# Sorting by source in three regions instead of two: the sums of tiles 124 to 255 beside the scatter

## The reference

```python
edge_aggr = zeros.at[row].add(edge_attr).at[col].add(edge_attr)   # layer 0: by source and by destination
agg = jax.ops.segment_sum(edge_attr, col, num_segments=N)         # layer 1: by destination
deg = jax.ops.segment_sum(ones, dst, num_segments=N)              # layers 2 and 3: counts
```

## Time and profile before

| | us |
|---|---|
| median of 3 runs | 1297.22 (1295.68 to 1298.08) |
| the profiled execution | 1292.79 |
| its span, first to last instruction | 1290.9 |
| PE busy | 1191.1 (92%) |
| DVE busy | 886.6 (69%) |
| POOL busy | 695.7 (54%) |
| ACT busy | 658.3 (51%) |

### The profile page before, as it was taken

The page is one execution under the profiler, slowest core; times in us unless marked ns, Lnnn a source line. Parts: engine busy times, 40 slices in busy tenths (PEclk is TensorE's granted clock), DMA queues, the critical chain, the costliest instruction groups (busy, mean ns, idle before and its releaser), DMA issues. The chain is left out here.

```text
span 1290.9 us, 34734 instructions
## 1 busy us (share of the span) xinstructions
PE 1191.1 (92%) x10908; PEld 1027.0 (80%) x10909; DVE 886.6 (69%) x3055; ACT 658.3 (51%) x1751; POOL 695.7 (54%) x720
## 2 busy tenths in 40 slices
PE   6999888999999999678986999997999999999997
PEld 3666556888988888567864999855999999999986
DVE  7999686667777677677778753473667766766753
ACT  8666447777778775379632310051333333333332
POOL 4777777777777777700000000037677777777740
PEclk9999898999999999989998999987999999999997
DMA  8663334454454447168860000058888988888830
GB/s 250 209 224 102 104 110 123 120 145 132 132 142 127 128 130 205 54 177 241 259 41 39 1 2 2 1 162 206 205 214 207 230 211 208 214 209 220 207 93 29
DMA packets 249761, 187.56 MB, mean 145 GB/s; under 512 B 44682, under 2 KB 226433, under 8 KB 249441
## 3 DMA queue, kind: packets, MB, share of 16 engines
q1 hardware_dynamic: 214650, 135.70, 40.9%
q0 software_dynamic: 22656, 46.87, 12.2%
q10 hardware_dynamic: 12264, 2.70, 1.1%
HBM read 139.64 MB, written 43.62 MB: 142 GB/s over the span
## 5 line engine op out<-in xcount | busy, mean ns | idle before, releaser
L2504 POOL DMA_INDIRECT between<-p_table,src_g x292 | 285.7, 978 | 407.9 <-DMA p_table<-n_nm 308.5
L929 POOL DMA_INDIRECT rows_by_block<-h_t,mean_bc x312 | 303.9, 974 | 105.3 <-issue 88.0
L444 PE MATMUL acc<-ones_b 128*128 128x128 bf16 (+1 forms) x2024 | 226.6, 257 | 31.8 <-PEq L864 17.5
L1049 DVE TENSOR_TENSOR between<-between,acc 128x600 f32 x208 | 161.7, 778 | 115.9 <-PE acc L1154 105.8
L2646 ACT ACTIVATE between<-acc 128x384 f32<-128x384 f32 (+2 forms) x156 | 72.6, 465 | 253.9 <-PE acc L2768 199.7
L444 PEld LDWEIGHTS acc<-ones_b 128*128 128x128 bf16 x2024 | 134.1, 99 | 60.8 <-issue 42.5
L1143 PE MATMUL acc<-n_nm 128*128 128x384 bf16 (+1 forms) x832 | 142.8, 295 | 13.4 <-DVE n_nm L1013 7.0
L1013 DVE TENSOR_SCALAR n_nm<-iota_w,agg_sum 128x600 bf16<-128x600 f16 x416 | 142.7, 384 | 0.0
L950 ACT ACTIVATE away<-iota_b,agg_sum 128x128 bf16<-128x128 bf16 x416 | 140.9, 385 | 0.0
L2751 PE MATMUL acc<-w_msg,between 128*128 128x128 f32 x584 | 127.8, 301 | 0.0
L1143 PEld LDWEIGHTS acc<-n_nm 128*128 128x128 bf16 x832 | 74.0, 98 | 61.3 <-DVE n_nm L1013 11.3
(11 more groups left out here) (275 smaller groups left out, 2690.0 us busy)
## 6 DMA issues: line engine op xcount, KB each, us to landing
h_t<-in_edge_attr SPq DMA_DIRECT2D x78, 256.0 KB
between<-in_edge_attr SPq DMA_DIRECT2D x36, 512.0 KB
h_t<-rows_by_block SPq DMA_DIRECT2D x57, 195.0 KB, 2.9
h_t<-rows_by_block SPq DMA_DIRECT2D x41, 260.0 KB, 3.4
between<-in_dst SPq DMA_DIRECT2D x36, 288.0 KB
n_nm<-rows_by_block SPq DMA_DIRECT2D x69, 130.0 KB
by_dst<-q_whole_table SPq DMA_DIRECT2D x138, 64.0 KB
x_nm<-rows_by_block SPq DMA_DIRECT2D x30, 260.0 KB, 3.4
```

Of the source, the lines that this page charges most:

```text
L444: pe.matmul(acc[:, bank * BANK + skip:(bank + 1) * BANK].rearrange("p (a n) -> p a n", n=P), ones_b[:, :], ones_b[:, :].rearrange("p (a n) ...
L929: pool.indirect_dma_start(rows_by_block, bass.IndirectOffsetOnAxis(ap=place_in_table[:, t:t + 1], axis=0), row_group(g)[:, j, :], None).th ...
L1049: dve.tensor_tensor(between[:, :, bass.ds(first, W)], between[:, :, bass.ds(first, W)], acc[:, o:o + NB * WS].rearrange("p (b w) -> p b w" ...
L2504: pool.indirect_dma_start(got[:, q, j * D:(j + 1) * D], None, p_table, bass.IndirectOffsetOnAxis(ap=src_g[:, n * G + j:n * G + j + 1], axi ...
```

## The change

- The second region is split. Tiles 124 to 255 go to a middle region (`cap_mid`: 7 tiles of room for blocks 7 to 14, 6 for others, 3 for the last; 155 in all), tiles 256 to 415 to a late region (`cap1`: 7 or 8 tiles, 4 for the last; 181 in all). Two or three tiles at the end of each stretch are zeroed, by seven DMAs instead of four, before group 31.
- The middle region is summed inside the scatter stage too. There are 64 early reads: the 39 wide ones at pairs 78 to 144, then one for each of the 25 blocks at pairs 148 to 197 with up to seven tiles and 128 columns. Three read buffers instead of two. One-hots come two pairs after the read, every third read's on DVE in one instruction, the others' on ACT as before; sums four pairs after; a finished sum is taken five pairs after, by ACT for superblocks, and by DVE for middle blocks with an add into `held`.
- The filling matmuls beside sums fall from 12 to 4 a pair (64 to 17 on each 32nd), and run until the last pair.
- After the last pair, ACT checks 4 blocks' counts and DVE 2 blocks', so that 19 are left for ACT in the sum stage. DVE takes the statistics of `x` there (25 instructions).
- SP loads `x` and then the weights after the last early sum, instead of the weights at group 8 and `x` at group 100. The one-hot buffers of the early sums lie in the weights' memory.
- The sum stage has 49 reads of 181 tiles. DVE adds up the findings at read 46, PE's matmuls for flags stand after read 47, DVE makes the flags at read 48 (the last), and PE's product of weights follows the last read.

```diff
+def cap_mid(b):
+    return 7 if 7 <= b < 15 else 6 if b < NB - 1 else 3
 def cap1(b):
-    return 13 if b < 7 else 14 if b < NB - 1 else 6
+    return 7 if b < 15 else 8 if b < NB - 1 else 4
-EB_IN = 2
+EB_IN = 3
-EARLY_READ = 40
+HOTS_AFTER, SUM_AFTER, TAKE_AFTER = 2, 4, 5
+CHECKED_EARLY, CHECKED_BY_DVE = 4, 2
...
+            for b in range(NB):
+                reads.append((NSB + b, base_mid(b), cap_mid(b), True, True))
...
-            read_at_group = {EARLY_READ + r * 7 // 5: r for r in range(len(early_reads))}
+            read_pairs = {(78 + r * 68 // wide_reads if r < wide_reads else 148 + (r - wide_reads) * 52 // NB): r for r in range(len(early_reads))}
+            def by_dve(r):
+                return r % 3 == 2
...
-                        if g == ROWG:
-                            load_rest(sp)
...
-                        if g == GROUPS - 4:
-                            sp.wait_ge(vec.h, vec.at(1))
-                            sp.wait_ge(nodes_summed.h, nodes_summed.at(len(early_reads)))
-                            sp.wait_ge(kept.h, kept.at(len(early_reads)))
-                            sp.dma_start(x_nm[:, 0:NB - 1, :], x[0:(NB - 1) * P, :].rearrange("(b p) f -> p b f", p=P)).then_inc(loaded.h, 16)
+                        for i in range(g * PG, (g + 1) * PG):
+                            if i in read_pairs:
+                                early_read(read_pairs[i])
+                    sp.wait_ge(vec.h, vec.at(1))
+                    sp.wait_ge(nodes_summed.h, nodes_summed.at(len(early_reads)))
+                    sp.wait_ge(kept.h, kept.at(wide_reads))
+                    sp.dma_start(x_nm[:, 0:NB - 1, :], x[0:(NB - 1) * P, :].rearrange("(b p) f -> p b f", p=P)).then_inc(loaded.h, 16)
+                    sp.dma_start(x_nm[0:NLAST, NB - 1, :], x[(NB - 1) * P:N, :]).then_inc(loaded.h, 16)
+                    load_rest(sp)
                     sp.wait_ge(loaded.h, loaded.at(16 * 23))
...
+                    act.wait_ge(taken.h, taken.at(PAIRS))
+                    for b in range(CHECKED_EARLY):
+                        check_counts(act, b, b)
...
+                    def early_where(r):
+                        k, n = early_reads[r][2], early_width(r)
+                        dve.wait_ge(block_in[r % EB_IN].h, block_in[r % EB_IN].at(16 * (r // EB_IN + 1)))
+                        if r >= EB_HOT:
+                            dve.wait_ge(nodes_summed.h, nodes_summed.at(r + 1 - EB_HOT))
+                        dve.tensor_tensor(early_hots_of(r), iota_w[:, 0:n].rearrange("p (a n) -> p a n", a=1).broadcast_to([P, k, n]),
+                                          early_rows[:, r % EB_IN, 0:k, D:D + 1].broadcast_to([P, k, n]), ALU.is_equal).then_inc(nodes_hot.h, 1)
+                    def add_sum(r):
+                        c = (early_reads[r][0] - NSB) * P
+                        w = min(P, NSB * SBN - c)
+                        dve.wait_ge(nodes_summed.h, nodes_summed.at(r + 1))
+                        dve.tensor_tensor(held[:, c:c + w], held[:, c:c + w], acc[:, EARLY_AT:EARLY_AT + w], ALU.add).then_inc(agg_read.h, 1)
...
+                    dve.wait_ge(taken.h, taken.at(PAIRS))
+                    for b in range(CHECKED_EARLY, CHECKED_EARLY + CHECKED_BY_DVE):
+                        last = dve.tensor_scalar(junk_dve[:, b - CHECKED_EARLY, :], between[:, b, :], LIMIT, 0.0, ALU.is_gt, ALU.add, accum_out=excess[:, b:b + 1])
+                    last.then_inc(vec.h, 1)
+                    dve.wait_ge(loaded.h, loaded.at(16 * 23))
+                    for b in range(NB):
+                        dve.bn_stats(stats[:, b, :], x_nm[:, b, :])
...
                         if first_sum <= i < after_sums:
-                            stream_ones(pe, at_bank(i) // BANK + 1, 4 * warm, 3 * P)
+                            stream_ones(pe, at_bank(i) // BANK + 1, warm + 1, 3 * P)
...
-                        if r == 82:
-                            dve.wait_ge(checked.h, checked.at(NB))
+                        if r == 46:
+                            dve.wait_ge(checked.h, checked.at(NB - CHECKED_EARLY - CHECKED_BY_DVE))
                             dve.tensor_reduce(odd[:, 2:3], excess[:, :], AX.X, ALU.add).then_inc(late.h, 1)
-                        if r == 87:
+                        if r == 48:
                             dve.wait_ge(upd_turned.h, upd_turned.at(1))
...
-                    for b in range(NB):
-                        act.activation(junk[:, :], between[:, b, :], ACT.Relu, bias=low_bound[:, :], accum_out=excess[:, b:b + 1]).then_inc(checked.h, 1)
-                        if b < NB - 1:
-                            act.wait_ge(checked.h, checked.at(b + 1))
+                    for b in range(CHECKED_EARLY + CHECKED_BY_DVE, NB):
+                        check_counts(act, b, b - CHECKED_EARLY - CHECKED_BY_DVE)
```

More of the change, by code:

```diff
@@ L294, in build @@
         bases = sb("bases", [1, 2, NK])
-        over = sb("over", [1, 4, NB])
+        over = Space(n_flat[:, 2944:NP], F32).take([1, 6, NB])
         rel2 = sb("rel2", [P, TILES_HERE])
@@ L819, in reads_by_source @@
             for b in range(NB):
[L820 to L824, removed]
+                for j in range(0, cap1(b), LR):
+                    reads.append((b, base1(b) + j, min(LR, cap1(b) - j), j == 0, j + LR >= cap1(b)))
             return reads
@@ L829, in load_by_source, with check_counts @@
             sp.dma_start(rows_in_block[:, q, 0:k, :], rows_by_block[row * P:(row + k) * P, :].rearrange("(p j) w -> p j w", j=k)).then_inc(block_in[q].h, 16)
+        def check_counts(act, b, done):
+            if done > 0:
+                act.wait_ge(checked.h, checked.at(done))
+            act.activation(junk[:, :], between[:, b, :], ACT.Relu, bias=low_bound[:, :], accum_out=excess[:, b:b + 1]).then_inc(checked.h, 1)
         def place_and_count():
@@ L983, in _ @@
                         lows(i)
-                        r = early_of_pair(i - 3)
+                        r = early_of_pair(i - TAKE_AFTER)
+                        if r is not None and r < wide_reads and early_reads[r][4]:
+                            take_sum(early_reads[r][0])
+                        r = early_of_pair(i - HOTS_AFTER)
                         if r is not None:
-                            keep_keys(r)
-                        r = early_of_pair(i - 6)
-                        if r is not None and early_reads[r][4]:
-                            take_sum(early_reads[r][0])
+                            if not by_dve(r):
+                                early_where(r)
+                            if r < wide_reads:
+                                keep_keys(r)
                         g = i // PG
@@ L1073, in _ @@
                             own_rank(g + 1)
+                        r = early_of_pair(i - TAKE_AFTER)
+                        if r is not None and r >= wide_reads:
+                            add_sum(r)
+                        r = early_of_pair(i - HOTS_AFTER)
+                        if r is not None and by_dve(r):
+                            early_where(r)
                         if i == 4 * ROWG * PG:
```

189 lines of the change are left out of this document (114 added, 75 removed).

## The result

The changed kernel took **1274.53 us** (median of 4 runs, 1273.93 to 1278.34) against 1296.45 for the kernel before: a ratio of 0.9826 (0.9803 to 0.9848). That is 21.9 us less by the medians and 22.6 by the ratio. The forecast was 1265.5: inside the range and on the right side, but 9 us short. The profiled execution took 1278.34 us (span 1276.5), the longest of the four; that of before, 1292.79, is shorter than each of its four timed ones. So a stage that differs between the two profiles may differ less in the medians.

A forecast was written before the change was run, and what follows sets the result against it. POOL's indirect-DMA issue rate bounds the scatter stage; the sum stage behind it pays. -32.0 (sum stage) +0.3 (start) +0 = -31.7 us, so 1261.1 profiled and 1265.5 forecast as median, range 1260 to 1281.

The forecast's parts named there:

- The sum stage: Stage after the scatter stage: 181 tiles instead of 335, ending at 621.9 instead of 653.9 us, -32.0 us.
- four candidates: What ends the sum stage, counted from 555.5 us: PE 604, DMA 606, DVE 608, ACT's checks last at 614.1.
- The tail: Sum stage after ACT's last check: 4.1 us from reduce to product's copy, then 3.75 to the next stage's first DVE instruction.
- The scatter stage's lead: Collections ahead of POOL's scatters, 9 pairs or 23 us at 201.6 us: covers the added work, above 2 pairs all along.
- the PE sum: PE's time a pair in the scatter stage: filler falls from 13.4 to 4.4, giving 2.38 us wide, 2.13 late.
- the rival in which the lead runs out: Scatter stage: pairs with sums take 2.85 us, POOL waits 14 us or the end's work is late; 1268 to 1283, chance 0.22.
- POOL: Scatter stage: POOL stays at its issue rate, 2.54 us a pair, other engines covered by the lead; cost 0.
- By this rule the new one-hots would stop POOL: Scatter stage: shared-port rule for two-SBUF-input DVE instructions, set aside because POOL's issue spacing was 1.27 us in both stretches.
- The rival: Scatter stage: POOL is held by DVE's 21 new one-hots, each added in full, +18.5 us, 1284; chance 0.03.
- the prediction's own signs: Right if POOL's last issue is still at 550; wrong if the sum stage's first check starts after 556, among others.
- The stage's end: End of the scatter stage: early checks, statistics and weight loads all done before 555.5 us, margin 2.6 us; cost 0.
- The start: Kernel start: three more 26-element DVE instructions ahead of its first casts, +0.3 us; moving the weight loads, 0.

The follow-up runs named there:

- the full filler: Changed kernel with the filling matmuls beside sums back at 12 a pair (64 on each 32nd): 1293.2 us, 0.9965 of the kernel before.
- both repairs: Changed kernel with one-input compares on DVE for the early one-hots and nine early checks on ACT instead of four: 1258.9 us, 0.9709 of the kernel before.
- The one-input form: Changed kernel with DVE's early one-hots as one compare per tile, the key a scalar per partition: 1267.9 us, 0.9761 of the kernel before.

## Why the prediction was right in sign and too high in size

By the profiled execution the forecast was 1261.1 and the result 1278.3. The 17.2 us between are all found: start +1.1, POOL +6.8, sum stage +1.8, the rest +7.5.

**The sum stage** (forecast -32.0, measured -30.2). Of the four candidates ACT came last as worked out: the last check ended 58.5 us after the first, forecast 58.6. (The 3.09 us for a check is right, but it is the spacing of the checks; 78.7/25 would be 3.15, as the 78.7 hold ACT's other work, too.) DVE's wait at read 46 was 7.9 us instead of 0 to 6: the other candidates were counted to the last of 49 reads, and the wait stands two reads ahead of it (50.7 us after the first check, where I had DVE at 52.5 for all). The tail took 9.6 us instead of 7.85: its pieces came from a PE at full clock, and I had let PE stand idle without asking at what clock it would come back. The run with nine early checks showed the step: there the wait is gone, the matmuls take 1.16 us, and the tail 7.9 us.

**The scatter stage's lead** (forecast: kept). It stayed at 8 to 9 pairs, some 20 us. The filler carried it, as the PE sum said; the full filler brings the rival in which the lead runs out, and with it 18.6 us more (1293.2-1274.5). For that rival I had put a pair at 2.85 us; it was 2.91.

**POOL** (forecast 0, measured +6.8 us: 538.6 from first to last issue, before 531.8; against the repeat of before, 532.8, it is 5.8). This is **the step that failed**: "By this rule the new one-hots would stop POOL; the trace speaks against it." The rule of the Trainium skill (SBUF — State Buffer, "SBUF: two separate sides") was right on these one-hots, and the trace now agrees: 0.96 us grows to 1.79 beside a two-input instruction of 1.15 us. (The issue reads `mean_bc` from SBUF.)

What misled me was an average. The rows compare stretches with more and less DVE work by the spacing of the issues, 1.27 us in both, but the two-input instructions from SBUF in them last 0.26 to 0.35 us each and lengthen a single issue by 0.2 us at most. None of the 0.65 to 1.16 us that the change adds was in them. Yet the trace of before does hold the effect, issue by issue. From its timeline, first beside a two-input instruction, then beside two one-hots of line 1013 (one tensor and a key per partition):

```profile
218.24 0.35 DVE L1006 TENSOR_TENSOR agg_sum<-iota,place_w 128x192 f32<-128x192 f32 x1
218.28 1.15 POOL L929 DMA_INDIRECT rows_by_block<-agg_sum,mean_bc  x1 [0.30 <-issue]
...
475.65 0.65 DVE L1013 TENSOR_SCALAR n_nm<-iota_w,agg_sum 128x600 bf16<-128x600 f16 x2
476.00 1.13 POOL L929 DMA_INDIRECT rows_by_block<-h_t,mean_bc  x1 [0.30 <-issue]
```

The issues end 0.84 and 0.83 us after the DVE instructions, as the thirteen long ones of the changed kernel do. Of the 60 issues over 1.0 us in this trace 58 end 0.81 to 0.88 us after such an instruction, 6 of them after line 1006 and 52 after line 1013; all 60 together are 5.7 us over 0.96 us each. So the trace did not speak against the rule. The spacing of many issues couldn't show it; the end of single ones could.

The rival had the mechanism at a chance of 0.03, and the wrong price: it added all 18.5 us, where 6.8 were paid, because an issue waits only for what is left of a one-hot, and 8 of the 21 held none over 1.2 us. That the result still lies inside the range is in part luck: the range reached to 1281 for the sake of a lead that runs out, and the lead held. Two of the prediction's own signs did show: POOL's last issue came at 558.15 instead of 550, and the sum stage's first check at 563.8, after 556.

**The stage's end** (forecast 0, measured 0). DVE's checks took 3.47 us (3.4 taken), the statistics ended at 549.5 (552.9 taken), all under POOL's last issues.

**The start** (forecast +0.3). PE's opening stream began 0.34 us later, 11.11 for 10.77. But it took 5.30 us instead of 4.06 for the same twelve matmuls, at a granted clock that reads 1.00 in both profiles; why is open. In the repeats it took 5.15 us in the kernel before and 4.16 to 5.30 in changed ones, so this second part is not the change's.

**The rest** was no term of the forecast. It reads +7.5 us in the two profiles (644.5 for 637.0), most of it in the first layers, at a lower granted clock. Across the nine experiments these layers took 66.0 us for the kernel before and 67.3 to 79.4 for changed ones (67.3 for the kernel with both repairs). What sets them is open; filling the tail's wait didn't change them. With POOL +6.8, the sum stage +1.8 and about 1 of the start, 9.6 us are explained of the 9 by which the medians missed, so little of this part can stand in the medians. The one-input form, which removes POOL's term alone, came out at 0.9761, which is 1266.2 us by the median of 1297.2 that the forecast started from, less than a us from the forecast; the interval is 4.5 us to either side.

## What to carry to other kernels

Before you put work of DVE beside indirect DMAs that POOL issues, look at how long its single instructions run and what they read. Here an issue that began beside a long instruction with two tensors in SBUF waited until that ended. Split into several short ones with a key per partition, the same work lengthened no issue by more than 0.1 us in its run, even though it takes longer in all. When a rule and a trace seem to disagree, first see that the trace holds an instruction of the size in question, and look at single instructions before averages. And when a stage's bound is removed, look at the next one in line: here five checks moved ahead were worth nearly as much as the issues' delay.

## What the runs showed of the hardware that was not expected

- An indirect DMA's issue on POOL (0.96 us) that begins beside a DVE instruction with two tensors in SBUF is held until that ends, and ends 0.83 to 0.84 us after it: it took up to 1.94 us with 42 of them. Over a stage it cost 0.27 to 0.38 us for each us of such instructions, at 1.27 us between issues.
- A DVE compare of one tensor with a key per partition from SBUF holds an issue in the same way. In the kernel before, 52 issues of 1.00 to 1.14 us ended 0.81 to 0.88 us after a one-hot of line 1013 (0.37 us).
- DVE's long check with one tensor and a constant (line 1187, 3.47 us over 3200 bytes a partition) ran beside POOL's issues with no effect on them, and so did its sums with one input in PSUM (0.78 us).
- Waiting may go the other way, too. In the scatter stage of the kernel before, 69 of the 416 instructions of line 1013 end 0.10 to 0.13 us after an issue does, and they last up to 0.57 us where the median is 0.37. And in the trace of before, the timeline of its start:

```profile
4.04 2.52 DVE L557 TENSOR_SCALAR mean_bc<-iota 1x26 f32<-1x26 f32 x1
...
4.28 2.31 DVE L560 TENSOR_SCALAR part_high<-part 128x1 f32<-128x1 f32 x1
...
4.10 2.43 POOL L524 MEMSET between<- 128x2800 f32 x1 [2.13 <-DVE iota_w L554]
```

  DVE instructions that have 26 elements and less stand for 2.3 to 2.5 us and end when POOL's memset of 2.43 us does. The Trainium skill (SBUF — State Buffer, "SBUF: two separate sides") says that whichever of the two engines starts first keeps the shared ports for its whole instruction, where DVE's instruction has two inputs in SBUF or runs in a mode that uses two ports. These have one input, no row shows their mode, and the first of them starts 0.06 us before the memset. No run here took the two apart, so the cause is argued, not shown.
- The same matmuls of the first layers took 66 to 79 us, with the granted clock between 0.87 and 0.76, in kernels that differ only in the stages before.
